# A transformer tower on one Trainium2 core: the order of work within a step of the attention layers

## The reference

```python
h = _L0_tok_ref(x)
h = h + _L0_attn_ref(_layernorm(h, axis=-1), wq, wk, wv, wo)    # 32 heads of 16, 8 for k and v, rotary
h = h + _L0_ffn_ref(_layernorm(h, axis=-1), w1, w3, w2)
h = h + _L1_attn_ref(_layernorm(h, axis=-1), Wq, Wk, Wv, Wo)    # 16 heads of 32, 4 for k and v, ALiBi
h = h + _L1_ffn_ref(_layernorm(h, axis=-1), gate_up_packed, gate_up_scales, down_packed, down_scales)
```

## Time and profile before

| what | value |
|---|---|
| median of 3 runs | 2553.61 us (2553.13 to 2556.82) |
| the profiled execution: time | 2557.45 us |
| the profiled execution: span | 2555.6 us |
| busy share of the span | PE 89%, DVE 68%, ACT 57%, POOL 38% |
| attention, layer 0 | about 570 to 985 us of the span |
| attention, layer 1 | about 1575 to 1925 us of the span |

### The profile page before, as it was taken

One profiled execution on the slowest core, in us unless ns is written; L12 is line 12 of the kernel. 1 busy time (PEld: TensorE's weight loads), 2 busy tenths in 40 slices (PEclk: granted clock), 3 DMA queues, 4 the chain that ended last, 5 costly groups with the idle time before them and its releaser, 6 DMA issues. The chain is left out here.

```text
span 2555.6 us, 43703 instructions
## 1 busy us (share of the span) xinstructions
PE 2271.4 (89%) x13188; PEld 1137.9 (45%) x13188; DVE 1736.8 (68%) x2922; ACT 1445.6 (57%) x2310; POOL 979.5 (38%) x997
## 2 busy tenths in 40 slices
PE   7999999947999996389999995999996899999997
PEld 2333333315666663134444442666662344444443
DVE  6666666636888885575444683677766888788873
ACT  4666666635666664475222561666654666666663
POOL 2222222216666672042000360444433545455552
PEclk9999999978999997699999997999998999999999
DMA  4554545433322211122111223222211111111101
GB/s 120 131 133 132 131 129 132 116 98 134 107 65 64 63 54 34 40 72 82 55 53 49 83 87 103 67 81 79 79 62 42 34 38 50 38 45 46 42 26 50
DMA packets 144174, 194.53 MB, mean 76 GB/s; under 512 B 32549, under 2 KB 76165, under 8 KB 144058
## 3 DMA queue, kind: packets, MB, share of 16 engines
q1 hardware_dynamic: 117434, 159.58, 20.7%
q10 hardware_dynamic: 26624, 33.56, 4.8%
HBM read 125.17 MB, written 42.21 MB: 65 GB/s over the span
## 5 line engine op out<-in xcount | busy, mean ns | idle before, releaser
L330 DVE TENSOR_REDUCE tm_negmax<-tm_s 128x1 f32<-128x512 f32 x512 | 323.3, 679 | 167.7 <-PE tm_s L374 167.5
L291 ACT ACTIVATE tm_prob<-tm_s 128x1024 f32<-128x1024 f32 x256 | 257.5, 1023 | 141.2 <-PE tm_s L394 136.6
L1985 PE MATMUL f_part<-f_xhi,gu 128*128 128x512 f16 x704 | 270.2, 384 | 14.5 <-ACT f_firstg L1806 4.3
L1985 PE MATMUL f_part<-f_xlo,gu 128*128 128x512 f16 x704 | 269.6, 383 | 0.0
L411 PE MATMUL tm_o<-tm_prob,tm_vt 128*64 128x512 f32 x1024 | 255.4, 620 | 0.0
L2007 PE MATMUL f_pz<-dn,f_ghi 128*128 128x512 f16 x704 | 216.4, 383 | 27.4 <-ACT f_zc L1838 27.4
L1775 POOL TENSOR_TENSOR f_firstg<-f_firstg,f_secondg 128x512 f32<-128x512 f32 x88 | 148.6, 1688 | 198.6 <-DVE f_secondg L1881 198.6
L374 PE MATMUL tm_s<-tm_qk 96*128 96x512 f16 x512 | 199.3, 392 | 14.6 <-DMA tm_qk<-tm_xs 14.1
L394 PE MATMUL tm_s<-tm_qk 98*128 98x512 f16 x512 | 194.4, 383 | 0.9 <-DMA tm_qk<-tm_mrow 0.9
L248 POOL TENSOR_TENSOR tm_hn<-tm_nd,tm_rows 128x1024 f32<-128x1024 f32 x32 | 75.2, 2350 | 310.1 <-DMA tm_rows<-rden 310.1
L955 PE MATMUL a_bankB<-a_wqkv,a_xhi 128*128 128x512 f16 x512 | 158.5, 392 | 3.4 <-DVE a_xlo L805 3.3
(11 more groups left out here) (187 smaller groups left out, 5733.5 us busy)
## 6 DMA issues: line engine op xcount, KB each, us to landing
tm_qk<-tm_xs SPq DMA_DIRECT2D x384, 64.0 KB, 2.1
tm_xqk<-in_qk ACTq DMA_DIRECT2D x32, 512.0 KB, 4.6
a_hin<-h SPq DMA_DIRECT2D x64, 256.0 KB, 2.6
a_hres<-h SPq DMA_DIRECT2D x64, 256.0 KB, 2.7
h<-a_hout SPq DMA_DIRECT2D x64, 256.0 KB, 2.0
f_hin<-h SPq DMA_DIRECT2D x64, 256.0 KB, 2.8
f_hres<-h SPq DMA_DIRECT2D x64, 256.0 KB, 2.8
tm_vt<-in_vt ACTq DMA_DIRECT2D x32, 256.0 KB, 2.9
```

The lines of the kernel that those rows point to most:

```text
L291: nc.scalar.activation(prob[b][:, 2 * h:2 * h + 2, :], s2[:, i % 2, :, :], ACT.Exp, scale=SCALE).then_inc(exp_done, 1)
L330: nc.vector.tensor_reduce(negmax[u][:, m:m + 1], s1[:, p % BANKS, :], AX.X, ALU.max, negate=True).then_inc(s1_read, 1)
L1985: last = nc.tensor.matmul(part[q % BANKS][:, :], (gate, up)[which][:, j, m * P:(m + 1) * P], xparts[x][u][:, j, :], start=x == 0, stop=x == 1)
```

## The change

Nothing is added or removed, except that in layer 1 the wait for `kv_copied` now stands before `k_hi` alone. In GpSimd's step `values(n + 1)` goes from the front to the end. In VectorE's step the three statistics of tile n+4 go to the front, and `k_lo`, which stood near the end as `k_lo(n + 2)`, stands right behind them as `k_lo(n + 1)`. In ScalarE's step `qk_hi` is cut into `q_hi` and `k_hi`, with `x_hi(n + 3)` between them.

```diff
--- before.py
+++ after.py
@@ -619,13 +619,13 @@
 
             def step(k, u):
                 n = 2 * k + u
-                values(n + 1, 1 - u)
                 inverse_deviation(n + 4, u)
                 cross(n + 2, u, 0)
                 rotate(n + 2, 0)
                 cross(n + 2, u, 1)
                 rotate(n + 2, 1)
                 q_lo(n + 2, u)
+                values(n + 1, 1 - u)
             loop_pairs(pool, step, FIRST, FROM, TO, LAST)
 
         @block.scalar
@@ -703,19 +703,25 @@
                                    bankA[:, :].rearrange("p (b r q) -> p b r q", b=B, r=R))\
                         .then_inc(s["yThi_done"], 1)
 
-            def qk_hi(t, u):
+            def q_hi(t, u):
                 if inside(t, TILES):
                     if rope:
                         wait(act, s["rot_done"], 2 * t + 1)
                     else:
                         wait(act, s["q_copied"], t + 1)
-                        wait(act, s["kv_copied"], t + 1)
                     wait(act, s["kT_ready"], t)
                     src = rot if rope else qkv[u]
                     nc.scalar.copy(qs[:, :, :, 0, :], src[:, 0:DQ].rearrange("p (h r d) -> p r h d", h=HKV, r=R))\
                         .then_inc(s["qhi_done"], 1)
+
+            def k_hi(t, u):
+                if inside(t, TILES):
                     if rope:
                         wait(act, s["rot_done"], 2 * t + 2)
+                    else:
+                        wait(act, s["kv_copied"], t + 1)
+                    wait(act, s["kT_ready"], t)
+                    src = rot if rope else qkv[u]
                     nc.scalar.copy(kp[:, 0, :, :, :], src[:, DQ:DQ + DKV].rearrange("p (h d) -> p h d", h=HKV)
                                    .unsqueeze(2).broadcast_to([P, HKV, 2, D])).then_inc(s["khi_done"], 1)
 
@@ -731,8 +737,9 @@
                     copy_q(n + 2, u)
                 copy_kv(n + 2, u)
                 probs_hi(n)
-                qk_hi(n + 2, u)
+                q_hi(n + 2, u)
                 x_hi(n + 3, 1 - u)
+                k_hi(n + 2, u)
             loop_pairs(act, step, FIRST, FROM, TO, LAST)
 
         @block.vector
@@ -858,22 +865,22 @@
 
             def step(k, u):
                 n = 2 * k + u
+                if inside(n + 4, TILES):
+                    wait(dve, h_in[u], 16 * (k + 3))
+                row_stats(n + 4, u)
+                mean_variance(n + 4, u)
+                variance_eps(n + 4, u)
+                k_lo(n + 1, 1 - u)
                 residual(n - 2, u, k - 1)
                 maxes(n)
                 inverse_sums(n - 1)
                 normalise(n - 1)
                 shift(n)
-                if inside(n + 4, TILES):
-                    wait(dve, h_in[u], 16 * (k + 3))
-                row_stats(n + 4, u)
-                mean_variance(n + 4, u)
-                variance_eps(n + 4, u)
                 turn(n + 2, u, 0)
                 y_lo(n - 1)
                 turn(n + 2, u, 1)
                 x_normalised(n + 4, u)
                 probs_lo(n)
-                k_lo(n + 2, u)
                 x_lo(n + 3, 1 - u)
             loop_pairs(dve, step, FIRST, FROM, TO, LAST)
```

## The result

The changed kernel takes 2560.82 us (median of 17 runs, 2557.26 to 2563.03), the kernel before 2556.82 us (17 runs on the same chips, 2552.27 to 2560.09). The ratio is 1.0015, with a 95% interval of 1.0008 to 1.0021: 4.0 us slower by the medians, inside the 0.2% called no change, where 9.1 us less was forecast. The profiled execution took 2560.85 us, with a span of 2558.9 us.

What follows compares the result with a forecast made beforehand. Layer 0 was taken as bound by a ring of waits, layer 1 by TensorE. Layer 0's -10.6 us and layer 1's +1.5 sum to -9.1, from 2553.6 to 2544.5 us; range 2535 to 2558.

Steps and rivals of the forecast that it cites:

- the ring: Layer 0's loop: statistics, `rstd`, rotations, k's high part and `k_lo` wait on each other, 12.65 us; the change breaks it.
- the new wait: Layer 0's loop: TensorE waits 0.5 us a step for `k_lo`, held by `vhi` and ending 0.28 behind it.
- `k_lo` was not free: Rival, chance 0.15: `k_lo` is not held; layer 0's step 11.7, layer 1 costs nothing, 2535 us.
- did not need its 0.41 behind the release: Rival, chance 0.12: `k_lo` begins only when GpSimd ends, some 0.42 instead of 0.28 behind; 2552 us, no change.
- did not lose to `vrest`: Rival, chance 0.10: GpSimd takes `vrest` before VectorE is let in, `k_lo` ends at least 0.45 later; 2568 us.
- The rotation of q now ends at 2.62 + 0.37 + 1.27 = 4.26: Layer 0's loop, us from `copy_q`: rotation undisturbed at 1.27, with `xn` held by it until 4.54.
- For the unrolled steps I take nothing: Layer 0's steps outside the loop: no gain counted, as their waits are cheaper and nearer the floor of 11.58 us.
- is hidden under TensorE: Layer 1: beyond a wait of about 0.05 us in 30 steps, +1.5 us, the change costs nothing there.
- `values` starting late: Rival, chance 0.11: waits before `v16` make `vhi` end 0.24 later; layer 0 -5.3, layer 1 +8.7 us; 2557, no change.
- The slower one: Rival, chance 0.10: `k_lo` loses twice; layer 0 gains nothing (22 x 0.03), layer 1 waits 0.5 a step, +14, 2568 us.

Runs made afterwards that it cites:

- `xn` early: The changed kernel with VectorE's `x_normalised(n + 4)` moved right behind `shift`; 2552.21 us, ratio 0.9986 to the kernel before.
- the kernel with the unrolled steps repaired: The changed kernel with `k_hi` and `k_lo` at their old place in layer 1's unrolled steps ahead of the loop; 2554.92 us, ratio 0.9994.
- layer 1 alone: The changed kernel with the new order in layer 1 only, layer 0 in its old order; 2564.02 us, ratio 1.0028 to the kernel before.
- the values put back: The changed kernel with GpSimd's `values` at the front of its step again, in both layers; 2545.41 us, ratio 0.9957 to the kernel before.

## Why the prediction was wrong

The forecast was 9.1 us less, the medians give 4.0 more. Of the 13.1 between them, 7.3 lie in layer 0 (10.6 forecast, 3.3 measured) and 5.0 in layer 1 (+1.5 forecast, +6.5 measured); the rest is within what the untouched stretches move by.

**Right in kind: the ring and the new wait.** The statistics in front free `rstd`, GpSimd starts on q at once, the wait for `q_lo` goes, and one for `a_kp` comes. `k_lo` was to end 0.28 behind `vhi` and did so, in both layers. That VectorE asked for it in the middle of `vhi` was in part luck: it did so 7.54 behind `copy_q`, where 7.5 was forecast, but `xn` was over at 3.50 and not at 4.54. What that saved went into two waits for ScalarE that the forecast did not have, 0.4 for `probs_hi` and 0.7 for `x_hi` (`a_xlo` in the waits of the changed kernel); `x_hi` stands behind `q_hi`, which waits for the rotation of q. None of the rivals on this point came about: `k_lo` was not free, did not need its 0.41 behind the release, and did not lose to `vrest`. The Trainium skill (SBUF — State Buffer, Who interferes with whom) has the second to issue blocked until the first is done; the held `k_lo` ended 0.28 after the release and took 0.41 alone, so the trace shows that it waits, and less than its whole length behind the wait.

**Wrong: "The rotation of q now ends at 2.62 + 0.37 + 1.27 = 4.26".** I took `xn` to be held by the rotation, as at 609.14 in the earlier trace rows, and put the rotation at its undisturbed 1.27. Which of the two is held hangs on a margin that I did not work out for the new step. In the earlier trace rows the row of `xn` also starts first, by 0.06 us, and `xn` is held; in the new step it starts first by 0.12, and the rotation, which is on the path, pays. Whether the order turns between these two leads, or goes by something else (the steps of the earlier trace rows are unrolled), no run shows. By the lead, a forecast of both starts to better than 0.1 us would have been needed. Working the step through from `copy_q` at 892.49:

| from `copy_q` on | forecast | measured |
|---|---|---|
| cross products of q end | 2.62 | 2.71 |
| rotation of q ends | 4.26 | 4.61 |
| `q_lo` ends | 6.75 | 7.11 |
| `vhi` ends | 7.99 | 8.35 |
| `k_lo` ends | 8.27 | 8.63 |
| TensorE turns k | 8.33 | 8.68 |
| next `copy_q` | 12.09 | 12.53 |

Of the 0.44 here, 0.09 is there by the crosses (not followed further), another 0.26 comes with the rotation, and 0.09 behind the transposes (in the next step 0.01). That the 0.26 is `xn`'s doing is shown by the run with `xn` early. Against a step of 12.57, a step of 12.50 leaves 22 x 0.07 = 1.5 us; from `hout` the old step reads 12.60, which makes it 2.2. That leaves 1.1 for the unrolled steps of layer 0, which I took at nothing; the same code of layer 0 moves by as much from one profile to the next (441.0 to 442.2).

**Wrong: "For the unrolled steps I take nothing", as used for layer 1.** Of that layer I said that everything else "is hidden under TensorE". That holds in the loop, where the window of the earlier trace rows has TensorE busy for the whole 160 us, and there the forecast stands: 0.07 a step against 0.05. It was a reading of the loop alone. In the unrolled steps TensorE is busy for 4.2 to 4.8 us of 6 (the windows of the kernel before), it comes to k early, and `k_lo` ends at 1593.78, 1.75 us behind its high part, with `x_lo` and the statistics between the two. That the place of `k_hi` and `k_lo` makes the 5.5 us is shown by putting it back there alone.

How they divide can be read from the turnings of k, against the kernel with the unrolled steps repaired. The first comes 0.57 us later behind the layer's first load (its wait is 0.70). The window to the second is 0.85 longer, at the full clock, by a wait of 0.89. The next has such a wait and a stretch at the lower clock, and is 2.36 longer. The last has the lower clock alone and is 1.55 longer, or 1.65 against the kernel with `xn` early. So the clock costs 1.5 to 1.65 us each time, some 3.1 together, and the waits some 2.3 (my estimates from these rows), 5.3 in all. With `k_hi` and `k_lo` put back, the falls of the clock are gone together with the waits. But not every wait brings one, and why the kernel with `xn` early had one fall where the change had two stays open.

**Of the rivals**, the one nearest in size (2557, `values` starting late) was not what happened: `v16` starts at 899.55, 0.05 before `q_lo`'s end, as forecast. The slower one had its place right (TensorE waiting for `k_lo` in layer 1) and its cause wrong: in the loop it waits for a few hundredths, and the several tenths stand in the unrolled steps, with `x_lo` and the statistics in front of `k_lo`, and only some 0.4 us of GpSimd's. Its step for layer 0, 12.57 - 0.03 = 12.54, is the measured 12.53 by chance: `k_lo` got in behind `vhi` and not behind `vrest`.

## What to carry to other kernels

When a piece of work is moved, work out for every operation on the path who asks for the shared memory first in the new order, and with what margin: a lead of 0.12 us, where 0.06 had not been enough, put 0.26 us on the critical path 22 times. Where the margin can't be worked out so finely, cost both cases. Read the unrolled steps at the ends of a pipeline as a stage of their own; the loop's cover ("TensorE is full") doesn't hold there, and a move that costs 0.07 us a step in the loop cost 5.5 us ahead of it. A short wait there can also cost the clock, which by my estimate was the larger part of the 5.5. And when a change moves three things at once, try them one at a time: one of the three ate most of what the others gave, and the sum looked like nothing.

## What the runs showed of the hardware

- A VectorE operation held by a GpSimd one needs less than its own length behind the release: `k_lo` of 128x256 ended 0.28 us after `vhi` or `q_lo`, and took 0.41 alone.
- It goes the other way too: GpSimd's rotation took 1.53 instead of 1.27 when a VectorE operation of 0.54 was 0.12 ahead of it, and `v16` 0.53 instead of 0.29 with `k_lo` 0.03 ahead.
- The row that starts first is not always the one that gets through: at 609.14 in the earlier trace rows `xn` starts 0.06 ahead of the rotation and is held (1.60), and 0.12 ahead, in the loop of the changed kernel, it is not (0.54).
- Three waits of 0.70 to 0.89 us, in a stretch where TensorE is not full anyway, stood beside windows with a mean granted clock between 0.72 and 0.94, where the same stretch without them had 1.00 throughout. It was so in each of the four kernels that had these waits (the change, layer 1 alone, the values put back, `xn` early) and in none of the six without. One such fall of the clock cost 1.65 us between two kernels that were the same up to it, to 0.01 us.
